# Statistics and rows of later quads on ScalarE, batch 1's candidate counts as pairwise sums, in a cross-attention and expert-choice kernel

## What is computed

```python
x = x + tanh(g_xattn[0]) * xattn(layernorm(x), ctx, mask, Wq, bq, Wk, bk, Wv, bv, Wo, bo)
x = x + tanh(g_ffn[0]) * ffn(layernorm(x), gate_w, w1, w2)

def ffn(x, gate_w, w1, w2):            # x: 2 batches x 2048 tokens x 512
    probs = softmax(einsum('ntd,ed->nte', x, gate_w))       # 8 experts
    g, m = top_k(probs.transpose(0, 2, 1), 512)             # each expert picks 512 tokens of a batch
    xin = x[batch_idx, m]
    h = gelu(einsum('nekd,edf->nekf', xin, w1))             # 512 -> 2048
    h = einsum('nekf,efd->nekd', h, w2)                     # 2048 -> 512
    return zeros.at[batch_idx, m].add(g[..., None] * h)
```

## Time and profile before

| | |
|---|---|
| median of 3 runs | 1535.75 us (1533.82 to 1538.56) |
| profiled execution | 1535.88 us, span 1534.1 us |
| busy: PE, PEld | 1490.6 us (97%), 1226.1 us (80%) |
| busy: DVE, ACT, POOL | 995.7 us (65%), 726.4 us (47%), 576.4 us (38%) |
| mean granted TensorE clock | 0.994 of full |

### The profile page before, as it was taken

One profiled execution on the slowest core, in us unless ns is written; L12 is line 12 of the kernel. 1 busy time (PEld: TensorE's weight loads), 2 busy tenths in 40 slices (PEclk: granted clock), 3 DMA queues, 4 the chain that ended last, 5 costly groups with the idle time before them and its releaser, 6 DMA issues.

```text
span 1534.1 us, 20306 instructions
## 1 busy us (share of the span) xinstructions
PE 1490.6 (97%) x7329; PEld 1226.1 (80%) x7329; DVE 995.7 (65%) x1727; ACT 726.4 (47%) x1278; POOL 576.4 (38%) x544
## 2 busy tenths in 40 slices
PE   7987899999999999999999999999999999999997
PEld 7755677888888888888888888888888888888886
DVE  3678775558767666676667666666667575766543
ACT  2245633455545554455445544545445444554532
POOL 2263554625443244404442344313441444323311
PEclk9999899999999999999999999999999999999999
DMA  7274624624233423233324433342424432342133
GB/s 234 80 257 172 210 86 131 165 83 102 91 110 75 118 74 119 60 106 83 110 87 92 98 109 93 80 109 77 124 58 103 102 107 87 82 110 82 42 76 76
DMA packets 101386, 163.37 MB, mean 106 GB/s; under 512 B 7411, under 2 KB 45315, under 8 KB 101285
## 3 DMA queue, kind: packets, MB, share of 16 engines
q1 hardware_dynamic: 86672, 128.16, 26.6%
q0 software_dynamic: 14400, 33.56, 11.4%
q10 hardware_dynamic: 213, 0.34, 0.1%
HBM read 128.48 MB, written 33.55 MB: 106 GB/s over the span
## 4 chain that ended last, share of the span: by engine, by line
PE 86%; DVE 3%; ACT 1%; issue 1%; DMA 1%; POOL 0%; POOLq 0%; DVEq 0%; ACTq 0%
PE bank L1457 44%; PE bank L1343 35%; PE bank L1319 4%; PE bank L1636 2%; DVE atleast L1028 0%; PE bank L1506 0%; DVE count L976 0%; PE bank L600 0%; DMA xg<-xn_rows,slot_source 0%; DVE x L880 0%; ACT spare L664 0%; DMA layer_out<-y,slot_row 0%; ACT xn L728 0%; ACT hid L1329 0%; DVE hid_low L1335 0%
## 5 line engine op out<-in xcount | busy, mean ns | idle before, releaser
L1457 PE MATMUL bank<-w2hl,hh 128*128 128x512 f32 x2024 | 628.4, 392 | 0.4 <-DVE hid_low L1335 0.4
L1343 PE MATMUL bank<-xo,whl 128*128 128x512 f32 x2352 | 541.6, 389 | 0.1
L1343 PEld LDWEIGHTS bank<-xo,whl 128*128 128x128 f32 x2352 | 441.2, 188 | 92.5 <-issue 0.5
L1457 PEld LDWEIGHTS bank<-w2hl,hh 128*128 128x128 f32 x2024 | 375.8, 188 | 75.9 <-DVE hid_low L1335 0.9
L1457 PE MATMUL bank<-w2hl,hid_low 128*128 128x512 f32 x1012 | 394.0, 389 | 0.0
L1457 PEld LDWEIGHTS bank<-w2hl,hid_low 128*128 128x128 f32 x1012 | 189.9, 188 | 39.6
L1583 POOL DMA_INDIRECT layer_out<-y,slot_row x64 | 104.7, 1637 | 295.0 <-ACT y L1496 279.6
L1273 POOL TENSOR_TENSOR whl<-raw,whl 128x512 fp32r<-128x512 f32 x56 | 81.3, 1453 | 258.1 <-ACT whl L1236 258.1
L1304 DVE TENSOR_TENSOR w2hl<-raw,w2hl 128x512 fp32r<-128x512 f32 x213 | 148.6, 720 | 38.6 <-ACT w2hl L1299 38.6
L1299 ACT ACTIVATE w2hl<-raw 128x512 fp32r<-128x512 f32 x228 | 136.5, 624 | 60.8 <-DMA raw<-in_L_ffn_w 33.5
L1278 POOL TENSOR_TENSOR whl<-wsum,whl 128x512 fp32r<-128x512 f32 x56 | 73.0, 1304 | 183.4 <-ACT whl L1257 183.4
(11 more groups left out here) (240 smaller groups left out, 1756.5 us busy)
## 6 DMA issues: line engine op xcount, KB each, us to landing
raw<-in_L_ffn_w SPq DMA_DIRECT2D x228, 256.0 KB, 2.7
raw<-in_L_ffn_w SPq DMA_DIRECT2D x72, 512.0 KB, 4.9
x_s<-in_x SPq DMA_DIRECT2D x8, 1024.0 KB, 9.6
layer_out<-x SPq DMA_DIRECT2D x8, 1024.0 KB, 9.3
xn_rows<-xn SPq DMA_DIRECT2D x8, 1024.0 KB, 5.3
raw_k<-in_L_xattn_Wk SPq DMA_DIRECT2D x1, 1024.0 KB, 6.5
raw_q<-in_L_xattn_Wq SPq DMA_DIRECT2D x1, 1024.0 KB, 8.6
raw_v<-in_L_xattn_Wv SPq DMA_DIRECT2D x1, 1024.0 KB, 11.4
```

What stands on the lines that cost most here:

```text
L1343: last = pe.matmul(bk[:, :], whl[:, p % 2, part, 2 * w + k, :], xo[:, xpart, x, k, :], start=(not adds and k == 0 and part == HIGH and xpa ...
L1457: last = pe.matmul(Y_BANKS[c][:, :], high if hpart == HIGH else low[:, c * P:(c + 1) * P], w2hl[:, f % 4, part, :], start=(s == 0 and hpar ...
```

## The change

**ScalarE takes quads 3 to 5.** LATE becomes 3, so quad 3 too has its mean from `x1sum` and its squares from ScalarE, and BN_STATS and BN_AGGR of quad 3 go. With ACT_ROWS = 3, the rows of quads 3, 4 and 5 are written by ScalarE (`rows_act`, three times 4 instructions), behind its squares of the next quad; GpSimd keeps quads 0 to 2. Semaphores follow (`act_rows`).

**Order where attention ends.** `logits_out(3)` and the start of batch 0's choice stand ahead of `weights_in` and `weigh` of quad 4. ScalarE makes w1's pair 1 high part already ahead of the exponentials of quad 7, its first token copy between two squares, and GELU of block 0 ahead of six row instructions in place of two ahead and four behind. VectorE takes over all early low parts: w1 pairs 0 and 1 in four halves between the `weigh` of quad 7, w2's blocks 0 and 1 ahead of the token splits.

**Batch 1's counts.** The reduce L976 becomes four additions: 8 tiles on 8, 4 on 4, 2 on 2, 1 on 1, in 16 bits. The count matmul moves from behind chunk c == 0 to behind c == 2.

**Gathers.** In block 12 they stand ahead of GpSimd's low parts.

```diff
-    LEAD, LATE = 3, 4
+    LEAD, LATE = 3, 3
+    ACT_ROWS = 3
...
+        def rows_act(act, q, tiles):
+
+            for i in tiles:
+                if i == 0:
+                    act.wait_ge(shifted2, q - ACT_ROWS + 1)
+                    wait(act, xn_out[q % 2], 16 * (q // 2))
+                act.activation(xn2[:, q % 2, i, :], x1[:, q % 2, i, :], ACT.Identity,
+                               scale=norm2[:, q % 2, 2, i:i + 1], bias=norm2[:, q % 2, 3, i:i + 1])\
+                   .then_inc(act_rows, 1)
...
                 if q == NQ - 1:
-                    w1_high_act(act, 0, 0, 0)
+                    for p in range(2):
+                        w1_high_act(act, 0, 0, p)
...
-                    w1_high_act(act, 0, 0, 1)
                 if LEAD <= q + 1 < NQ:
                     for i in range(Q):
                         square(q + 1, i)
+                if ACT_ROWS <= q - 1 < NQ - 2:
+                    rows_act(act, q - 1, range(Q))
...
-                weights_in(q)
-                weigh(q, 0)
                 if q == CHOOSE_FROM:
                     logits_out(q - 1)
                     choice_start_dve(dve, own, 0)
+                weights_in(q)
+                weigh(q, 0)
+                if q == NQ - 1:
+                    w1_low_half(dve, 0, 0, 0, 0)
                 weigh(q, 1)
...
-            w1_low_part(dve, 0, 0, 0)
+            w1_low_half(dve, 0, 0, 1, 1)
+            for f in range(2):
+                w2_low_sub(dve, 0, 0, f)
             split_tokens_dve(dve, 0, 0)
...
                 if b == 1:
-                    tile_counts(dve, count[:, :, :], atleast[:, :, :, :].rearrange("p c t e -> p c e t"))\
+
+                    half = TB // 2
+                    while half > 1:
+                        step(dve.tensor_tensor(atleast[:, :, 0:half, :], atleast[:, :, 0:half, :],
+                                               atleast[:, :, half:2 * half, :], ALU.add))
+                        half //= 2
+                    dve.tensor_tensor(count[:, :, :], atleast[:, :, 0, :], atleast[:, :, 1, :], ALU.add)\
                         .then_inc(bit_count, 1)
...
-                if c == 0 and inside is not None:
+                if c == 2 and inside is not None:
                     choice_pe(pe, 1, inside)
...
+                    if b == 0 and f == GATHER_1:
+                        for c in range(NC):
+                            gather_pool(pool, 0, 1, c)
+                        promote_pool(pool, 0, 1)
                     if w2_no(*next_block(b, f)) < W2_EARLY:
                         w2_low_sub(pool, *next_block(b, f))
                     if f % 2 == 0:
                         w1_low_part(pool, *next_pair(b, f))
-                    if b == 0 and f == GATHER_1:
-                        for c in range(NC):
-                            gather_pool(pool, 0, 1, c)
-                        promote_pool(pool, 0, 1)
```

More of the change, by code:

```diff
@@ L715, in attention_act @@
                         x_out(q + 2, i)
-            for i in range(Q):
+            for i in range(2):
                 square_x1(NQ - 1, i)
-            for c in range(NC):
+            first_tokens_act(act, 0)
+            for i in range(2, Q):
+                square_x1(NQ - 1, i)
+            for c in range(1, NC):
                 first_tokens_act(act, c)
[L722 to L730, removed]
         def attention_pool(pool):
@@ L804, in attention_pool @@
                     deviations(q)
[L805 to L809, removed]
+                    if q < ACT_ROWS:
+                        for i in range(Q):
+                            if i == Q // 2:
+                                first_deviations(it + 1)
+                            rows(q, i)
+                    else:
                         first_deviations(it + 1)
@@ L934, in attention_dve @@
                 weigh(q, 2)
+                if q == NQ - 1:
+                    w1_low_half(dve, 0, 0, 1, 0)
                 if q == NQ - 2:
@@ L1206, in wait_w2_low @@
             if isinstance(done, int) and done <= W2_EARLY:
-                wait(eng, w2_low_early, done)
+                wait(eng, w2_low_first, min(done, 2))
+                wait(eng, w2_low_early, done - 2)
             else:
@@ L1257, in w1_sum_high_act, with w1_low_half @@
             act.activation(whl[:, p % 2, HIGH, 2 * S1:14, :], wsum[:, :, :], ACT.Copy).then_inc(w1_sum_high, 1)
+        def w1_low_half(eng, e, b, p, half):
+            high, low = (whl[:, p % 2, part, 4 * half:4 * half + 4, :].rearrange("p i f -> p (i f)")
+                         for part in (HIGH, LOW))
+            if half == 0:
+                eng.wait_ge(w1_high, pair_no(e, b, p) + 1)
+            ins = eng.tensor_tensor(low, raw1[:, p % 2, 2 * half:2 * half + 2, :].rearrange("p k f -> p (k f)"),
+                                    high.bitcast(F32), ALU.subtract)
+            if half == 1:
+                ins.then_inc(w1_low, 1)
         def w1_low_part(pool, e, b, p):
-            if is_plain(e) and b == 0 and p == 1:
-                pool.wait_ge(w1_low, 1)
+            if is_plain(e) and b == 0 and p == 2:
+                pool.wait_ge(w1_low, 2)
             high, low = whl[:, p % 2, HIGH, :, :].bitcast(F32), whl[:, p % 2, LOW, :, :]
@@ L1266, in w1_low_part @@
                 for half in range(2):
-                    last = pool.tensor_tensor(low[:, 4 * half:4 * half + 4, :].rearrange("p i f -> p (i f)"),
-                                              raw1[:, p % 2, 2 * half:2 * half + 2, :].rearrange("p k f -> p (k f)"),
-                                              high[:, 4 * half:4 * half + 4, :].rearrange("p i f -> p (i f)"),
-                                              ALU.subtract)
-                last.then_inc(w1_low, 1)
+                    w1_low_half(pool, e, b, p, half)
             else:
@@ L1304, in w2_low_sub @@
             eng.tensor_tensor(w2hl[:, f % 4, LOW, :], raw2[:, slot, :], w2hl[:, f % 4, HIGH, :].bitcast(F32),
-                              ALU.subtract).then_inc(w2_low_early if eng is nc.gpsimd else w2_low, 1)
+                              ALU.subtract)\
+               .then_inc(w2_low_early if eng is nc.gpsimd else w2_low_first if is_plain(e) and w2_no(e, b, f) < 2
+                         else w2_low, 1)
         def hidden_pe(pe, b, f):
@@ L2049, in _ @@
             attention_act(act)
-            last_rows_act(act, NQ - 2, range(2))
+            rows_act(act, NQ - 2, range(2))
             choice_act(act, 1)
             act.activation(spare_gate[:, :], gates[:, 0:1], ACT.Gelu)
-            last_rows_act(act, NQ - 2, range(2, Q))
             act.wait_ge(added, Q * NQ)
             gelu_act(act, 0, 0)
-            last_rows_act(act, NQ - 1, range(Q))
+            rows_act(act, NQ - 2, range(2, Q))
+            rows_act(act, NQ - 1, range(Q))
             plain_act(act)
```

24 lines of the change are left out of this document (15 added, 9 removed).

## The result

The changed kernel takes 1543.58 us (median of seven executions), the kernel before 1535.75 in the same series. One of the seven took 3873.53 us and is left out of the ratio; the median of the other six is 1542.5. The ratio is 1.0041, 95% interval 1.0029 to 1.0054: 6.3 us slower. The profiled execution took 1541.37 us with a span of 1539.5, so the profile has +5.4 us of span to explain.

A forecast was written before the change was run, and what follows sets the result against it. PE was taken as the bound, with VectorE in the chain in quads 4 to 7. 1535.88 - 2.9 + 0.9 - 0.4 + 10.3 - 1.1 = 1542.7 us; range of 8 in 10 runs 1531 to 1546.

The forecast's parts named there:

- The lock and the five waits: Plain part: VectorE's additions take turns with GpSimd's low parts; five odd pieces keep PE waiting 11.9 us, net +10.3.
- first two rivals: Turns without second w2 low part: +4.4, 1536.8 us, chance 0.20; additions find gaps, no count late: 1530.8 us, chance 0.20.
- The test named ahead: Plain part: additions of 1.2 us and more where 0.2 to 0.4 is their own time would show the forecast right.
- That of the waits: Plain part: PE waits of 1.5 to 4 us each for the last addition in five odd pieces.
- Part 1: Quads 4 to 6: squares 0, rows off GpSimd -1.3 in iteration 5, `values_dve` -1.6 in iteration 6; sum -2.9 us.
- The zero for statistics against squares: Quad 4: ScalarE's squares delay the first `weigh` by about what VectorE saves on BN_STATS: 0, bounds -0.5 and +0.5.
- The bound of ScalarE's rows: Attention: quad 5's rows on ScalarE end about when quad 7's softmax input is ready, costing 0 to 1 us.
- The third rival: Quads 4 to 7: ScalarE becomes the bound, part 1 gives only -0.9, with full waits: 1544.7 us, chance 0.10.
- Part 2: End of attention: low parts on VectorE delay the first hidden product, +0.9; the wait for the first hidden block goes, -0.4.
- Part 4: Gather of batch 1: starts about 4 us earlier, so PE's 1.1 us wait for it goes, -1.1.

The follow-up runs named there:

- e10: e1 with quad 3's statistics again by VectorE's BN_STATS instead of ScalarE's squares: 1528.69 us, ratio 0.9951 to the kernel before.
- e8: e1 with the rows of quads 3 to 5 on GpSimd again: 1533.45 us, ratio 0.9991 to the kernel before.
- e7: e1 with the low parts of w2's blocks 0 and 1 and w1's pair 1 on GpSimd again: 1529.36 us, ratio 0.9962 to the kernel before.
- e1: The changed kernel with batch 1's counts again by the one reduce instead of four additions: 1528.66 us, ratio 0.9951 to the kernel before.
- e4: e1 with VectorE's token splits ahead of the hidden low part in blocks 14 and 15: 1528.89 us, ratio 0.9953 to the kernel before.
- e9: The changed kernel with GpSimd's low parts in the plain part replaced by memsets that read nothing: 1527.16 us, ratio 0.9945 to the kernel before.
- e6: e1 with the gather of batch 1 behind block 12's low parts again: 1529.79 us, ratio 0.9962 to the kernel before.
- e3: The changed kernel with only the first addition, then a reduce over the 8 sums: 1529.49 us, ratio 0.9954 to the kernel before.
- e11: e4 with block 14's w2 low part on VectorE moved behind block 15's splits: 1529.25 us, ratio 0.9952 to the kernel before.
- e2: The kernel before with only the four additions in place of the reduce: 1550.09 us, ratio 1.0090 to the kernel before.
- e5: The kernel before with only the count's matmul moved behind chunk 2 instead of chunk 0: 1534.77 us, ratio 0.9993 to the kernel before.

## Why the prediction came out right, step by step

**The lock and the five waits: right.** The forecast named pieces 1, 3, 5, 7 and 9, at 3.9, 1.6, 2.4, 2.0 and 2.0 us; the trace has 3.3, 1.2, 1.9, 1.6 and 1.6. Each is 0.4 to 0.6 short, 9.7 in place of 11.9. In block 2 the output starts at 185.19 and GpSimd's w2 part at 188.20, O + 3.0 as in the sum. The last addition ends at 194.15, which is O + 8.96, and the sum had 9.2. The difference is the third addition: GpSimd's second w2 part started only at 192.85, after 0.32 us of idle time, and let it through. The rows are VectorE's fourth addition and GpSimd's w2 part there, then the fourth addition of piece 5:

```profile
192.95 1.20 DVE L1060 TENSOR_TENSOR count<-atleast 128x56 bf16<-128x56 bf16 x1
...
192.85 1.26 POOL L1334 TENSOR_TENSOR w2hl<-raw,w2hl 128x512 fp32r<-128x512 f32 x1 [0.32 <-ACT w2hl L1329]
...
207.19 0.19 DVE L1060 TENSOR_TENSOR count<-atleast 128x56 bf16<-128x56 bf16 x1
```

Of the first two rivals neither came, since that w2 part did slip in, ahead of the fourth addition. The test named ahead, additions of 1.2 us and more, holds (3.83 us for three, 1.16 for the fourth). That of the waits, 1.5 to 4 us each, holds in four of the five; piece 3's is 1.22.

**The clock behind a long wait: missing.** The term's price was the wait alone. The 3.3 us wait cost another 1.4 to 1.7 us; the others, of 1.2 to 1.9 us, left no such stretch in the changed kernel (PE pairs of 0.71 us right behind the second, 1.00 granted for 4 us behind each). Only the sum of both, +9.5, is near the +10.3 that I had.

**Part 1 (-2.9): right in mechanism, and the trace shows more than it forecast.** Quad 5 (-1.3 forecast) moved by -1.25, and `values_dve` (-1.6) by -1.56. The zero for statistics against squares held in e10 as far as its time can tell, although exponentials of quad 4 came 2.7 us later, as said. The trace has two gains that the sum hasn't. One is quad 4 to 5: quad 5's softmax input comes 1.3 us earlier; e8 gives quad 3's rows 0.9 of that, and the rest is within what this interval varies. The other is about 0.9 in iteration 7, which cancels the +0.9 of part 2: in the changed kernel PE has waited 1.6 us and not 3.1 for VectorE, runs at a granted clock of 0.78 and not 0.61 in the next stretch, and reaches quad 7's first `weigh` sooner. The bound of ScalarE's rows (0 to +1) stood at its lower end. The third rival, ScalarE as the bound, is out.

**Part 2 (+0.9 and -0.4): right on the stretch, wrong on a reason.** e7 prices the low parts on VectorE at 0.7 us against e1, and the wait for the first hidden block went. But I wrote that freeing `logits_out(7)` of GpSimd moves only piece 0, "which nobody waits for". Behind piece 0 on VectorE stands block 0's hidden low part, and PE does wait for that: in e7, 1.8 us, and a stretch at the lower clock behind it. So by the traces the move pays for itself there: 0.7 us spent, 3.5 not lost.

**Part 4 (-1.1): wrong.** The gather's wait went, and 1.1 us came back 5 us later at the splits. I looked for who else is late on GpSimd, the engine that was reordered, and not for what stands behind the same tokens on VectorE.

**The sum.** -4.1 (forecast -2.0), -0.2 (-0.4), +8.1 and +1.4 (+10.3), 0 (-1.1), and 0.3 unassigned: +5.5 against +6.8. Two errors make the forecast too high (2.1 of gain missing in attention, 0.8 too much for the counts) and one too low (1.1 for the gather), so the total is nearer than its terms, and that much of the hit is luck. Without the additions the rest of the change is worth -7.5 us (e1), where my terms give -2.9 + 0.9 - 0.4 - 1.6 - 1.1 = -5.1.

One profile can't fix the attention terms more finely than that. e1, e4, e9, e6, e3, e11 and the changed kernel run the same program up to there, and their first hidden product stands at 157.9 to 162.0. The kernel before, e2 and e5 also share one program up to there, and have it at 164.7, 163.1 and 162.0. By the means of the seven and the three the gain is 3.3 us and not 4.1, against 2.0 forecast. The same window of quad 4 in e6, then in e1, shows one reason, the granted clock (0.53 against 0.93):

```profile
101.00:107.00 6.00, 5.28 (x6) 1.59 (x6) 3.29 (x13) 5.94 (x13) 2.46 (x3) 0.53 0.73 267
```

```profile
101.00:107.00 6.00, 3.92 (x23) 1.21 (x21) 5.24 (x20) 5.92 (x13) 2.50 (x4) 0.93 0.69 256
```

Why the clock differs between executions of one program there was not tried.

## What to carry to other kernels

Beside GpSimd instructions that read SBUF, price a VectorE instruction with two SBUF inputs at its own time plus the rest of GpSimd's, and again for each one that follows while GpSimd has more to do: splitting one long reduce into four short additions made it 1.2 us alone and 5.0 us in company. Take such work off the pair where its result is waited for, or give one of the two a form that doesn't share (a reduce, a write without a read). And when a wait is taken away, follow the data to its next user on every engine before booking the gain: here one wait of 1.1 us simply reappeared 5 us later.

## What the runs showed of the hardware that was not expected

A wait of PE can cost more than its length, and its length doesn't say whether it will. After 3.3 us (changed kernel) and 3.8 us (e2) without work the mean granted clock was 0.62 and 0.61 for the next 4 us and more. The waits of 1.2 to 1.9 us in the changed kernel left it at 1.00, and so did those of 2.95 and 2.70 us in e2. But about 1 us behind the wait of 1.8 us in e7 it fell to 0.50, and so it did behind the last wait of e2, 2.69 us. The windows are e7's and then e2's:

```profile
170.00:173.00 3.00, 3.00 (x10) 1.98 (x9) 0.67 (x2) 2.97 (x5) 0.00 (x0) 0.50 1.06 409
```

```profile
240.00:242.50 2.50, 2.50 (x8) 1.93 (x7) 2.14 (x7) 0.00 (x0) 0.00 (x0) 0.50 0.81 290
```

What decides it no run here isolates.

A GpSimd memset of a 128x512 tile (0.53 us) doesn't hold VectorE's two-input instructions, where the subtraction into the same tile (1.3 us) does. GpSimd pays as well: its w1 halves took 1.58 us on average beside the additions, against 1.27 where it runs two in a row.
